# Two tiles instead of one returned by one-hot products, and the shared expert's products re-banked and moved, in an AdaLN mixture-of-experts layer

## The reference

```python
logits = jnp.einsum('td,ed->te', x, router_w)
top_idx = jnp.argmax(logits, axis=-1)
score = jax.nn.sigmoid(jnp.max(logits, axis=-1))
xs = x * score[:, None]
h = silu(xs @ expert_gate[e]) * (xs @ expert_up[e])      # e = top_idx of the token
moe_out = h @ expert_down[e]
sh = (silu(x @ shared_gate) * (x @ shared_up)) @ shared_down
out = x_in + moe_out + sh                                 # x is the normed x_in
```

## Time and profile before

| | us |
|---|---|
| median of 3 runs (lowest, highest) | 63.3 (62.9, 63.58) |
| the profiled execution's own time | 62.81 |
| its span in the profile | 60.8 |
| TensorE, VectorE, ScalarE, GpSimd busy | 51.1, 30.7, 25.1, 26.8 |

### The profile page before, as it was taken

How to read it: one execution, slowest core, us unless ns; L and a number is a source line. 1 busy time by engine, 2 the same in 40 slices (tenths; PEclk the granted TensorE clock), 3 DMA queues, 4 the chain that set the end, 5 groups by cost and what they waited for, 6 DMA issues and landing times.

```text
span 60.8 us, 1140 instructions
## 1 busy us (share of the span) xinstructions
PE 51.1 (84%) x285; PEld 34.6 (57%) x285; DVE 30.7 (51%) x122; ACT 25.1 (41%) x72; POOL 26.8 (44%) x53
## 2 busy tenths in 40 slices
PE   2999999999999489997989999979999966995000
PEld 1318687777393044695936664746666655994000
DVE  3252386958736999913144244056554441538540
ACT  0932109599989403301233654355556552000000
POOL 4659960000277787660000576607556666600000
PEclk9999999999999999999999999999999999999955
DMA  0779999953999999921359201111100010107365
GB/s 0 208 230 253 378 422 414 411 231 89 327 384 370 347 411 406 369 71 43 86 148 231 57 5 43 36 43 30 45 6 22 9 43 23 43 20 240 105 191 154
DMA packets 6487, 10.55 MB, mean 174 GB/s; under 512 B 895, under 2 KB 4099, under 8 KB 6481
## 3 DMA queue, kind: packets, MB, share of 16 engines
q1 hardware_dynamic: 4989, 8.90, 42.6%
q0 software_dynamic: 640, 1.06, 5.3%
q10 hardware_dynamic: 852, 0.52, 2.7%
HBM read 6.26 MB, written 4.48 MB: 177 GB/s over the span
## 4 chain that ended last, share of the span: by engine, by line
PE 30%; issue 19%; POOL 16%; DMA 15%; ACT 7%; DVE 4%; SPq 1%; POOLq 1%; DVEq 1%; ACTq 0%
POOL y_tok L404 9%; PE bank L566 7%; POOL slots_x L394 7%; PE bank L425 6%; DMA y_back<-y_tok 5%; PE bank L596 5%; PE bank L436 5%; DMA slots_x<-x_rows,slot 4%; DMA y_tok<-y,slot_x 3%; DMA slot_x<-slots_x 3%; PE bank L442 3%; ACT L712 2%; PE bank L430 2%; ACT x_rows L695 1%; DVE stats L798 1%
## 5 line engine op out<-in xcount | busy, mean ns | idle before, releaser
L404 POOL DMA_INDIRECT y_tok<-y,slot_x x11 | 10.8, 984 | 13.7 <-DVE y L993 9.2
L394 POOL DMA_INDIRECT slots_x<-x_rows,slot x8 | 8.4, 1053 | 9.8 <-ACT x_rows L695 8.0
L566 PE MATMUL bank<-ex_w,exT 128*128 128x512 f32 (+1 forms) x22 | 11.4, 598 | 0.0
L596 PEld LDWEIGHTS bank<-ex_w,ehT 128*128 128x128 f32 x44 | 6.3, 190 | 6.9 <-issue 5.7
L491 PE MATMUL bank<-nT,sh_w 128*128 128x512 f32 (+1 forms) x18 | 8.0, 560 | 1.1 <-DVE hs L854 1.1
L993 DVE COPY y<-bank 128x128 f32<-128x128 f32 x12 | 3.5, 291 | 10.5 <-PE bank L596 8.0
L596 PE MATMUL bank<-ex_w,ehT 128*128 128x128 f32 (+1 forms) x44 | 7.1, 284 | 1.4 <-issue 0.9
L746 ACT ACTIVATE eg<-bank 128x256 f32<-128x256 f32 x12 | 4.6, 385 | 6.7 <-PE bank L566 5.0
L988 DVE TENSOR_TENSOR eh<-eg,bank 128x256 f32<-128x256 f32 x12 | 4.9, 412 | 2.4 <-ACT eg L746 2.4
L740 ACT ACTIVATE ehT<-bank 128x256 f32<-128x256 f32 x11 | 4.2, 383 | 4.5 <-PE bank L581 3.5
L734 ACT ACTIVATE exT<-bank 128x128 f32<-128x128 f32 x12 | 3.3, 274 | 4.0 <-PE bank L625 2.9
(11 more groups left out here) (108 smaller groups left out, 78.8 us busy)
## 6 DMA issues: line engine op xcount, KB each, us to landing
ex_w<-in_expert_w_dram SPq DMA_DIRECT2D x8, 384.0 KB
slots_x<-empty_rows SPq DMA_DIRECT2D x1, 1935.0 KB, 9.8
slots_x<-empty_rows SPq DMA_DIRECT2D x1, 645.0 KB, 11.0
slot_x<-slots_x SPq DMA_DIRECT2D x4, 129.0 KB, 2.5
xT<-in_x_cols_dram SPq DMA_DIRECT2D x2, 256.0 KB, 4.3
x_tok<-in_x_dram SPq DMA_DIRECT2D x1, 512.0 KB
sh_w<-in_shared_w_dram SPq DMA_DIRECT2D x1, 384.0 KB, 6.0
slot_x<-slots_x SPq DMA_DIRECT2D x4, 64.5 KB, 1.8
```

The costliest lines, as they stand in the source:

```text
L394: nc.gpsimd.indirect_dma_start(out=slots_x, out_offset=bass.IndirectOffsetOnAxis(ap=slot[:, b:b + 1], axis=0), in_=x_rows[:, b, :], in_off ...
L404: nc.gpsimd.indirect_dma_start(out=y_tok, out_offset=bass.IndirectOffsetOnAxis(ap=slot_x[:, tile, H:H + 1].bitcast(U32), axis=0), in_=y[:, ...
L566: last = nc.tensor.matmul(bank[EX_GU[i % 2]][:], exT[:, i % 2, :], ex_w[:, bass.ds(expert[i], 1), 0:2 * FF], start=True, stop=True)
L596: last = nc.tensor.matmul(bank[EX_Y[i % 2]][:, 0:H], hidden, ex_w[:, bass.ds(expert[i], 1), 2 * FF + k * H:2 * FF + (k + 1) * H], start=(k ...
```

## The change

It does four things. (1) The last two tiles of the order (6 and 7, `LASTS`) are put in token order by one-hot products instead of one. GpSimd writes two scatters of zeros ahead of all scatters of y and then ten of y; VectorE copies two columns of token numbers in turn 2 and makes eight `is_token` comparisons in turns 3 to 10; TensorE does sixteen one-hot products, in which those of tile 7 accumulate onto those of tile 6 in the same bank. (2) The four shared gate and up pairs use six banks, so the third pair and the fourth wait for less. (3) `shared_down` of batches 0 to 2 stands ahead of gate_up(0), of 3 to 5 behind it (`EARLY` = 6); gate_up(1) waits for the residuals of all six, and down(0) no longer waits for residuals. (4) `shared_down` of 6 and 7 stand ahead of down(10) and down(11).

```diff
-        SH_BANKS = [(0, 1), (7, 5)]
-        SH_Y = (4, 6, 2, 7, 0, 1, 4, 7)
+        SH_GATE, SH_UP = (0, 7, 4, 1), (1, 5, 0, 7)
+        SH_Y = (4, 6, 2, 7, 1, 4, 0, 1)
+
+        EARLY = GB + 2
...
             def tiles_out(run):
                 for i, tile in enumerate(run.tiles):
-                    if tile == LAST:
+                    if tile in LASTS:
                         break
...
-                    if run is main and i == 0:
-                        pool.wait_ge(slot_x_in[piece_of(LAST)], 16)
...
+            for tile in LASTS:
+                pool.wait_ge(slot_x_in[piece_of(tile)], 16)
+                nc.gpsimd.indirect_dma_start(out=y_tok, out_offset=row_numbers(tile), in_=zeros[:], in_offset=None,
+                                             bounds_check=T - 1, oob_is_err=False).then_inc(main.y_out, 16)
             tiles_out(main)
...
             def shared_up(i, u, first=0, end=GB):
                 g, k = i // K2, i % K2
-                if i >= 2:
-                    pe.wait_ge(hs_done, i - 1)
-                last = nc.tensor.matmul(bank[SH_BANKS[k][u]][:, first * S:end * S],
+                if i == 2 and u:
+                    pe.wait_ge(sg_done, 1)
+                if i == 3:
+                    pe.wait_ge(*((sg_done, 2) if u else (hs_done, 1)))
+                last = nc.tensor.matmul(bank[(SH_UP if u else SH_GATE)[i]][:, first * S:end * S],
...
             def shared_down(b):
-                pe.wait_ge(hs_done, K2 * (b // GB + 1))
-                if b == 3:
-                    pe.wait_ge(sg_done, 2 * K2)
+                pe.wait_ge(hs_done, 2 * K2 if b == 3 else K2 * (b // GB + 1))
+                if b == 0:
+                    pe.wait_ge(sg_done, K2 + 1)
+                if b == 5:
+                    pe.wait_ge(r_done, 1)
...
+                    if run is main and i == 1:
+                        pe.wait_ge(r_done, EARLY)
                     pe.wait_ge(run.exT_done, i + 1)
...
-                    if run is main and i == 0:
-                        pe.wait_ge(r_done, GB)
...
+                def fill(i):
+                    if run is main and i >= run.n - 2:
+                        shared_down(EARLY + i - (run.n - 2))
...
-                    for b in range(GB // 2, GB):
+                    for b in range(GB - 1, EARLY):
                         shared_down(b)
...
                     if i - 2 in run.turned:
+                        fill(i - 2)
                         down(i - 2)
...
-            for b in range(GB // 2):
+            for b in range(GB - 1):
                 shared_down(b)
...
-            for b in range(GB, B):
-                shared_down(b)
-            pe.wait_ge(main.y_done, main.n)
-            pe.wait_ge(is_token_done, B // 2)
-            for b in range(B):
...
+            pe.wait_ge(is_token_done, B)
+            for g in range(GROUPS):
+                for t, tile in enumerate(LASTS):
+                    if g == 0:
+                        pe.wait_ge(main.y_done, main.n - 1 + t)
+                    for b in range(GB):
+                        last = nc.tensor.matmul(last_place(g)[:, b * H:(b + 1) * H], is_token[:, t, g * GB + b, :], y[:, tile, :],
+                                                start=(t == 0 and b == 0), stop=(t == 1), skip_group_check=True)
+                last.then_inc(last_ps, 1)
...
-            for b in range(GB):
+            for b in range(EARLY):
                 residual(b)
...
+                    if run is main and i == 2:
+                        for t, tile in enumerate(LASTS):
+                            dve.wait_ge(slot_x_in[piece_of(tile)], 16)
+                            nc.vector.tensor_copy(last_tokens[:, t:t + 1], slot_x[:, tile, H:H + 1].bitcast(I32)
+                                                  ).then_inc(last_tokens_done, 1)
+                    if run is main and 3 <= i < 3 + B:
...
             expert_tiles(main)
-            for b in range(GB, B):
+            for b in range(EARLY, B):
                 residual(b)
```

More of the change, by code:

```diff
@@ L136, in adaln_moe_kernel @@
         token_at = sb("token_at", [P, B, S])
-        last_token = sb("last_token", [P, 1])
-        is_token = sb("is_token", [P, B, S])
+        last_tokens = sb("last_tokens", [P, 2])
+        is_token = sb("is_token", [P, 2, B, S])
         out_sb = sb("out_sb", [P, B, H])
@@ L194, in rare_in_use @@
             return engine.value_load(over_size[0:1, 0:1], min_val=0, max_val=OVER) > RARE
-        LAST = main.tiles[-1]
+        LASTS = main.tiles[-2:]
         def last_place(g):
@@ L396, in _, with row_numbers @@
                     in_=x_rows[:, b, :], in_offset=None).then_inc(x_out, 16)
+            def row_numbers(tile):
+                return bass.IndirectOffsetOnAxis(ap=slot_x[:, tile, H:H + 1].bitcast(U32), axis=0)
             def tiles_out(run):
                 for i, tile in enumerate(run.tiles):
-                    if tile == LAST:
+                    if tile in LASTS:
                         break
@@ L403, in tiles_out @@
                     pool.wait_ge(run.y_done, i + 1)
[L404 to L408, removed]
-                    if run is main and i == 0:
-                        pool.wait_ge(slot_x_in[piece_of(LAST)], 16)
[L411 to L414, removed]
+                    nc.gpsimd.indirect_dma_start(out=y_tok, out_offset=row_numbers(tile), in_=y[:, tile, :], in_offset=None,
+                                                 bounds_check=T - 1, oob_is_err=False).then_inc(run.y_out, 16)
+            for tile in LASTS:
+                pool.wait_ge(slot_x_in[piece_of(tile)], 16)
+                nc.gpsimd.indirect_dma_start(out=y_tok, out_offset=row_numbers(tile), in_=zeros[:], in_offset=None,
+                                             bounds_check=T - 1, oob_is_err=False).then_inc(main.y_out, 16)
             tiles_out(main)
@@ L689, in gate_silu @@
                     act.wait_ge(hs_done, i - 1)
-                nc.scalar.activation(sg[:, i % 2, :], bank[SH_BANKS[i % K2][0]][:], ACT.Silu).then_inc(sg_done, 1)
+                nc.scalar.activation(sg[:, i % 2, :], bank[SH_GATE[i]][:], ACT.Silu).then_inc(sg_done, 1)
             def scale_rows(b):
@@ L853, in shared_hidden @@
                 dve.wait_ge(su_ps, i + 1)
-                nc.vector.tensor_tensor(hs[:, k, g * GB * S:(g + 1) * GB * S], sg[:, i % 2, :], bank[SH_BANKS[k][1]][:],
+                nc.vector.tensor_tensor(hs[:, k, g * GB * S:(g + 1) * GB * S], sg[:, i % 2, :], bank[SH_UP[i]][:],
                                         ALU.mult).then_inc(hs_done, 1)
@@ L999, in expert_tiles @@
                         gated(i)
[L1000 to L1007 removed]
+                    if run is main and i == 2:
[4 more added lines that the diff above has]
+                    if run is main and 3 <= i < 3 + B:
+                        t, j = (i - 3) // (B // 2), (i - 3) % (B // 2)
+                        dve.wait_ge(last_tokens_done, t + 1)
+                        nc.vector.tensor_scalar(is_token[:, t, 2 * j:2 * j + 2, :], token_at[:, 2 * j:2 * j + 2, :],
+                                                last_tokens[:, t:t + 1], None, ALU.is_equal).then_inc(is_token_done, 1)
             expert_tiles(main)
[L1010 removed]
+            for b in range(EARLY, B):
                 residual(b)
```

14 lines of the change are left out of this document (1 added, 13 removed).

## The result

| | before | after |
|---|---|---|
| median of the runs, us | 63.35 (62.9 to 63.58, 4 runs) | 65.28 (65.11 to 65.89, 4 runs) |
| ratio, 95% interval | | 1.043 (1.036 to 1.049) |
| profiled execution: time, span | 62.81, 60.8 | 65.31, 63.6 |
| gate_up(1) starts | 31.04 | 31.61 |
| last down of the loop starts | 51.25 | 53.52 |

The kernel became slower by 4.3%, outside the forecast range. The two ends of the sum: the final additions start 1.83 later, and the stores behind them take 0.96 longer; what lies around the span is 0.3 shorter; together the 2.50 between the two profiled executions.

What follows compares the result with a forecast made beforehand. Bound: the routed rows' return, y_back, before the final additions at 57.00. These would start at 56.5, gaining 0.5: profiled 62.81 becomes 62.3, and with 0.5 for the runs' median 62.8 us; range 61.8 to 63.8.

Steps and rivals of the forecast that it cites:

- these late releases: TensorE results answered late before the change: exT read 0.9 late at 27.92, gate_up at 37.00 answered 1.0 late at 39.07.
- one might vanish: Rival: a late release of about 1 us goes away with the new order, time 61.8; chance 0.15.
- The scatter queue's own sum: GpSimd's last scatter moves 1.41 earlier to 50.31; back to back it could not start before 49.6, so the queue catches up.
- d = 0: Delay of gate_up(1) from shared downs moved ahead of tile 1: taken as 0, bounds 0 and 0.45.
- The idle 1.06: TensorE's 1.06 us wait ahead of 21.51 for hs goes with the new bank plan; four shared products end 1.06 sooner.
- If all that follows moves with them: Condition after the four shared products: gate_up(0) can then go at about 27.3 instead of 28.34, hiding the moved shared downs.
- No cover ahead of tile 1: Rival: moved shared downs delay gate_up(1) by 0.45, additions from 56.95, a gain of 0.05, time 63.2; chance 0.20.
- The slower rival: Rival: gate_up(1) waits for residual(5), tile 1 starts at 32.08, 1.04 late, additions at 57.5, time 63.8; chance 0.12.
- (b): TensorE's last one-hot products and VectorE's addition into r_rows: second addition stays at 55.57, takes 0.69, over at 56.26.
- The rival of held scatters: Rival: eight VectorE comparisons each delay a GpSimd scatter by 0.38, returned rows at 57.9, time 64.2; chance 0.03.
- From there four additions, the stores and the end take 3.8; the change touches none of that: From the first final addition at 57.00 to the span's end at 60.8: 3.8 us, unchanged.
- the forecast 56.5: Start of VectorE's first final addition after the change, instead of 57.00: a gain of 0.5; forecast's chance 0.50.

Runs made afterwards that it cites:

- a_dip: Changed kernel, y_tok zeroed by a plain DMA ahead of SyncE's wait for fill_most, replacing two scatters of zeros: 62.04 us, ratio 0.998 to 1.010.
- b_dip: Kernel before, y_tok zeroed by a plain DMA ahead of SyncE's wait for fill_most, replacing its scatter of zeros: 62.18 us, ratio 0.995 to 1.007.
- a_fill: Changed kernel, y_tok zeroed by one plain SyncE DMA behind the loads of ex_w, replacing two scatters of zeros: 63.22 us, ratio 0.998 to 1.014.
- b_fill: Kernel before, y_tok zeroed by one plain SyncE DMA behind the expert weights, replacing its scatter of zeros: 63.66 us, ratio 1.002 to 1.019.
- b_two: Kernel before plus two tiles by one-hot products and two scatters of zeros first, banks and order as before: 66.99 us, ratio 1.063.
- a_hold: Changed kernel with all ten scatters of y held back until the whole loop is done, the two of zeros staying early: 75.47 us.
- a_late: Changed kernel, y_tok zeroed by one plain SyncE DMA behind the loads of slot_x, replacing two scatters of zeros: 63.89 us, ratio 1.000 to 1.020.

## Why the prediction was wrong

**The step that failed first** is the sentence "I do not know the cause of these late releases; I assume that they stay". I had seen both, and priced only that one might vanish; no rival let them grow. What makes them longer is what the change adds. It puts a second scatter of zeros ahead of the row of y, four in a row become five or six, and the loop loses 2.70 instead of 1.00: a term of +1.70 that the sum did not have. The scatter queue's own sum was right (the last scatter at 50.3 + 2.27 = 52.57, measured 52.59), and was asked only whether the queue catches up, not what a fuller queue does to others.

**d = 0**: measured 0.57. The idle 1.06 did go and the products moved; "If all that follows moves with them" failed, since exT came no earlier: its release goes with the end of the row of scatters of x, not with its products. So the rival "No cover ahead of tile 1" is what happened, 0.44 for the third shared down behind gate_up(0) and 0.13 because exT came that much later. On the chip where nothing is late, exT is there at 25.17 in a_dip, but gate_up(0) then waits for ex_w until 27.88, a bound that my sum did not have. There gate_up(1) starts at 31.31 in a_dip, behind its shared downs, and at 31.70 in b_dip, behind slot_x; the two have different bounds, and whether the bank plan alone covers the moved shared downs stays open. The slower rival (the wait of gate_up(1) for residual(5)) had no part in 31.61: that row waits for exT.

```profile
25.17 0.28 ACT L745 ACTIVATE exT<-bank 128x128 f32<-128x128 f32 x1 [2.05 <-PE bank L635]
```

(ScalarE in a_dip: exT right behind its products.)

**The tail up to the final additions** held to a tenth: (b) does not move against the last down (55.57 + 2.27 = 57.84, measured 57.84), and the register load and branch put the final additions 0.99 behind the second addition's start, where I had 0.93. The two shared downs fit into TensorE's idle time and the comparisons cost nothing: without late releases the loop takes 19.22 with both (a_fill) and 19.21 with neither (b_fill, four comparisons). The rival of held scatters is out: 0.98 to 1.00 with eight comparisons, and 1.08 once. The exclusion that the Trainium skill tells of ("SBUF — State Buffer", "Who interferes with whom") is not seen in these rows; it is stated for a two-port mode, and no row shows whether the comparisons run in one.

**"From there four additions, the stores and the end take 3.8; the change touches none of that"** failed too: 4.77. The landing times of the four stores, before and after:

```profile
DMA to landing us min/median/max: 1.8/1.9/1.9
```

```profile
DMA to landing us min/median/max: 2.1/2.1/2.9
```

The trace's packets show an 8 KB load of instructions at 60.69, amid the stores, which in the kernel before comes at 62.58, after the end. In all thirteen profiles with two one-hot tiles it falls among the stores, which take 3.9 to 4.3 from first issue to the span's end; in all seven with one tile it comes after the end, and they take 3.3 to 3.5. The two sets of kernels differ in more than this, so it is a coincidence in twenty profiles, not an experiment; what the load is for and whether it holds the stores was not tried.

Together: the forecast 56.5 + 0.57 + 1.70 + 0.06 = 58.83 for the final additions, and 0.96 more on the stores. On the chip without late releases the change is worth about what is left: a_dip has its final additions at 55.84, b_dip at 56.92, 1.08 earlier, and pays 0.7 of it back behind them (4.66 against 3.98 to the span's end). Both take the time of the kernel before within 1%.

No version here was shown to beat the kernel before. By the table above a_dip and b_dip, with no scatters in a row in the loop, might on a chip of the usual kind; they did not run on one.

## What to carry to other kernels

A wait in the trace that ends late for no reason you can name is not a constant: ask what runs on the other engines at that moment, and whether the change makes that longer, before you carry the old delay into the sum. Count how many of GpSimd's scatters leave without a pause, not only when the last one leaves; a zero fill by a plain DMA takes scatters out of that row, if it is placed where it delays no load that is waited for. And measure the same kernel on a second chip before a difference of 2% is put down to an edit.

## What the runs showed of the hardware

- Results of TensorE were released late while GpSimd issued three or more indirect DMAs without a pause: a Silu 3.13 us after its product's start in the changed kernel and 4.40 in b_two, where 1.06 is usual, and exT 0.9 to 2.5 after its products were over. One by one at 1.63 us (a_fill), or two in a row (a_hold), they did no harm, nor did a plain fill of 512 KB beside the loop (a_late). Why is open.
- On five chips every kernel that lets scatters of y pile up shows this in its loop. On the sixth no release was late, even with six scatters in a row, and the kernel before takes 61.92 instead of 63.0 to 63.7.
- TensorE goes on meanwhile: in the changed kernel its shared downs start at 25.69, right behind the products whose result is read at 28.05. It stalls only where it needs an answer. As the ends of its records are modelled, the trace does not tell whether a product or only its signal is late.
- A last scatter landed in 2.1 to 2.3 us, and in 3.9 to 4.3 in the four profiles where a 16 KB load of instructions met it. Four stores of 128 KB landed in 1.9 us or in 2.1 to 2.9 us, with an 8 KB load among them in the slower case. Both are coincidences in the traces, not trials.
